# One core of Trainium2: a scan kernel whose B is broadcast over the partitions by one fp32 matmul in place of a bfloat16 matmul of three parts

## What is computed

```
u  = silu(conv4(x @ in_w_u) + conv_b)            # (512, 256)
z  = x @ in_w_z
dt8, B, C = split(u @ xproj_w.T)                 # (512, 8), (512, 16), (512, 16)
dt = softplus(dt8 @ dt_w.T + dt_b)               # (512, 256)
h[t, d, n] = exp(dt[t, d] * A[d, n]) * h[t-1, d, n] + dt[t, d] * B[t, n] * u[t, d]
y[t, d] = sum_n h[t, d, n] * C[t, n] + u[t, d] * D[d]
out = (y * silu(z)) @ out_w.T
```

## Time and profile before

| what | value |
|---|---|
| median of 3 runs | 493.03 us (490.91 to 496.62) |
| profiled execution | 496.12 us, span 494.3 us |
| mean granted TensorE clock | 0.914 of full speed |
| TensorE busy, matmuls | 410.5 us (83%) |
| VectorE busy | 422.3 us (85%) |
| ScalarE busy | 369.4 us (75%) |
| GpSimd busy | 404.3 us (82%) |

### The profile page before, as it was taken

The page is one execution under the profiler, slowest core; times in us unless marked ns, Lnnn a source line. Parts: engine busy times, 40 slices in busy tenths (PEclk is TensorE's granted clock), DMA queues, the critical chain, the costliest instruction groups (busy, mean ns, idle before and its releaser), DMA issues. The chain is left out here.

```text
span 494.3 us, 6553 instructions
## 1 busy us (share of the span) xinstructions
PE 410.5 (83%) x2200; PEld 276.7 (56%) x2200; DVE 422.3 (85%) x345; ACT 369.4 (75%) x719; POOL 404.3 (82%) x241
## 2 busy tenths in 40 slices
PE   1947995998699987989898998889998967798854
PEld 0335554664556574555655684555665845457643
DVE  3577997999989998988999879998999989899254
ACT  2298699679966969897889689898789786972040
POOL 1799689797988799988979899989899999958431
PEclk9967999998879998998999899999999895989778
DMA  8251242322241233222232314223322332210001
GB/s 238 87 196 46 86 110 82 110 85 91 64 146 47 90 108 107 86 91 65 85 108 100 112 50 107 86 92 106 108 86 107 79 106 93 70 42 2 0 1 42
DMA packets 17009, 43.48 MB, mean 88 GB/s; under 512 B 1616, under 2 KB 5968, under 8 KB 16976
## 3 DMA queue, kind: packets, MB, share of 16 engines
q1 hardware_dynamic: 16976, 43.06, 27.1%
HBM read 41.48 MB, written 1.57 MB: 87 GB/s over the span
## 5 line engine op out<-in xcount | busy, mean ns | idle before, releaser
L1020 POOL TENSOR_TENSOR hq<-hq,c_tiles 128x1024 f32<-128x1024 f32 x129 | 300.6, 2348 | 45.2 <-DVE hq L1147 42.7
L1147 DVE TENSOR_TENSOR_SCAN hq<-da,bb 128x1024 f32<-128x1024 f32 x113 | 255.9, 2280 | 10.0 <-PE bb L631 2.6
L650 PE MATMUL ysum<-wts,hq 128*128 128x128 f32 x1024 | 150.7, 295 | 18.5 <-POOL hq L1020 17.0
L816 ACT ACTIVATE da<-dt,neg_a 128x511 f32<-128x511 f32 x226 | 147.1, 711 | 7.1 <-DVE hq L1147 6.8
L650 PEld LDWEIGHTS ysum<-wts,hq 128*128 128x128 f32 x1024 | 122.9, 150 | 43.0 <-POOL hq L1020 24.3
L1128 DVE TENSOR_TENSOR bb<-bb,dtu 128x1024 f32<-128x1024 f32 x80 | 97.0, 1213 | 9.3 <-PE bb L604 5.8
L914 ACT ACTIVATE g<-dtu_t,bc_t 128x256 f32<-128x256 f32 x132 | 55.9, 497 | 0.0
L1147 DVE TENSOR_TENSOR_SCAN hq<-bb,dbu 128x1024 f32<-128x1024 f32 x15 | 34.3, 2286 | 13.4 <-ACT bb L827 6.3
L631 PE MATMUL bb<-wts,g 128*128 128x128 f32 x264 | 37.8, 290 | 9.1 <-ACT g L914 7.1
L631 PEld LDWEIGHTS bb<-wts,g 128*128 128x128 f32 x264 | 32.2, 150 | 18.5 <-issue 9.9
L604 PE MATMUL bb<-b_rows,pick 48*128 48x512 bf16 x76 | 30.4, 400 | 9.6 <-DVE hq L1147 9.6
(11 more groups left out here) (127 smaller groups left out, 500.1 us busy)
## 6 DMA issues: line engine op xcount, KB each, us to landing
c_tiles<-bc_rows_dram SPq DMA_DIRECT2D x64, 512.0 KB, 3.6
b_tiles<-bc_rows_dram SPq DMA_DIRECT2D x15, 256.0 KB, 4.4
wconv<-conv_taps_dram SPq DMA_DIRECT2D x2, 512.0 KB, 7.1
x_res<-x_dram SPq DMA_DIRECT2D x1, 768.0 KB, 9.2
out_dram<-o SPq DMA_DIRECT2D x3, 256.0 KB, 2.3
wts<-packed_dram SPq DMA_DIRECT2D x1, 584.0 KB, 10.2
hid<-w_ffn_dram SPq DMA_DIRECT2D x1, 576.0 KB, 8.6
bc_rows_dram<-xdbl SPq DMA_DIRECT2D x8, 64.0 KB, 3.1
```

The costliest lines, as they stand in the source:

```text
L650: mm = nc.tensor.matmul(ysum[:, h, block(b)], hq[:, i % H_RING, h, block(b)], ident, start=(first and b == 0), stop=(i % NS == NS - 1), is ...
L816: ins = nc.scalar.activation(da[:, i % DA_RING, h, 1:SEQ], dt[:, k % 2, h, 1:SEQ], ACT.Exp, scale=neg_a[:, c:c + 1])
L1020: nc.gpsimd.tensor_tensor(hq[:, i % H_RING, halves, :], hq[:, i % H_RING, halves, :], c_tiles[:, n % C_RING, i % 2, :].unsqueeze(1).broadc ...
L1147: nc.vector.tensor_tensor_scan(out=hq[:, i % H_RING].rearrange("p h t -> p (h t)"), data0=decay.rearrange("p h t -> p (h t)"), data1=dbu_t ...
```

## The change

`bcast` becomes, in all 80 plain steps, one fp32 matmul whose moving operand are the 16 rows of B in `xdbl` themselves, and whose stationary operand is column n of the first 16 rows of the fp32 identity, repeated 128 times. Stages `pick`, `split` and `b_rows` are gone on GpSimd, TensorE and ScalarE, with their tiles and semaphores, and so is the 16-column picker in the packed weights. `xdbl` now has two buffers, since the rows are read through the whole unit: the copy of unit k waits for the store of unit k-2 in place of k-1, and for the broadcasts of unit k-2.

```
                 if stage == "bcast":
                     i, = a
                     k, n = i // NS, i % NS
-                    if i == 0:
-                        was_read(pe, ("bc", k))
-                    if i == first_from_rows(k):
-                        was_read(pe, ("b_rows", k))
+                    was_read(pe, ("xproj", k))
                     if i >= BB_RING:
                         pe.wait_ge(s_scan, i - BB_RING + 1)
-                    if from_rows(i):
-
-                        mm = nc.tensor.matmul(bb[:, i % BB_RING, 1, :],
-                                              pick[0:PARTS * NS, n:n + 1].broadcast_to([PARTS * NS, P]),
-                                              b_rows[:, k % 2, :], start=True, stop=True)
-                    for b in () if from_rows(i) else range(BLK):
-                        mm = nc.tensor.matmul(bb[:, i % BB_RING, 1, block(b)],
-                                              bc_t[:, k % 2, b, ROW_B + n:ROW_B + n + 1].broadcast_to([P, P]),
-                                              ident, start=True, stop=True, is_transpose=True)
+                    mm = nc.tensor.matmul(bb[:, i % BB_RING, 1, :],
+                                          ident[0:NS, n:n + 1].broadcast_to([NS, P]),
+                                          xdbl[ROW_B:ROW_B + NS, k % 2, :], start=True, stop=True)
                     mm.then_inc(s_bcast, 1)
-                elif stage == "b_rows":
-                    k, = a
-                    pe.wait_ge(s_split, 4 * (k + 1))
-                    pe.wait_ge(s_pick, 1)
-                    may_write(pe, item)
-                    for b in range(BLK):
-                        mm = nc.tensor.matmul(scratch(item).bitcast(BF16)[0:PARTS * NS, block(b)],
-                                              b_parts[:, b].rearrange("p s n -> p (s n)"), ident16[:],
-                                              start=True, stop=True, is_transpose=True)
-                    signal_full(mm, item)
...
         if k == 0:
-            put(at, ("dtu_turn", 0, 0), ("dtu_turn", 0, 1), ("pick",), ("split", 0), ("turn", 0, 1))
-            put(at + 1, ("b_rows", 0))
+            put(at, ("dtu_turn", 0, 0), ("dtu_turn", 0, 1), ("turn", 0, 1))
...
-            put(at + then + 9, ("dt", n, 0), ("dt", n, 1), ("split", n), ("dtu", n))
+            put(at + then + 9, ("dt", n, 0), ("dt", n, 1), ("dtu", n))
...
-            put(at + (11 if ffn or k == 0 else 10), ("b_rows", n))
...
-                    if k >= 1:
-                        act.wait_ge(s_cst, 16 * k)
-                    signal_read(nc.scalar.activation(xdbl[0:XROWS, :], scratch(item)[0:XROWS, :], ACT.Copy), item)
+                    if k >= 2:
+                        act.wait_ge(s_cst, 16 * (k - 1))
+                        act.wait_ge(s_bcast, plain_steps(NS * (k - 1)))
+                    signal_read(nc.scalar.activation(xdbl[0:XROWS, k % 2, :], scratch(item)[0:XROWS, :], ACT.Copy), item)
...
-                elif stage == "split":
-
-                    k, = a
-                    was_read(pool, ("bc", k))
-                    if k >= 1:
-                        written(pool, ("b_rows", k - 1))
-                    b_t = bc_t[:, k % 2, :, ROW_B:ROW_B + NS]
-                    nc.gpsimd.tensor_copy(b_parts[:, :, 0, :], b_t).then_inc(s_split, 1)
...
```

More of the change, by code:

```diff
@@ L39 @@
 for _name, _n in (("ident", P), ("gamma", 1), ("beta", 1), ("conv_b", 4), ("skip", 4), ("a_log", 4 * NS),
-                  ("wx", 4 * XROWS), ("wdt", 2 * DI), ("rev", P), ("pick", NS), ("wz", 2 * DI), ("wo", 4 * DM)):
+                  ("wx", 4 * XROWS), ("wdt", 2 * DI), ("rev", P), ("wz", 2 * DI), ("wo", 4 * DM)):
     COLS[_name] = (_at, _at + _n)
@@ L47 @@
 G_RING = 2
-FIRST_ROWS = 4
-PARTS = 3
 TURNED = ((4, 6, 10, 13), (0, 4, 6, 10, 13)) + 3 * ((3, 6, 10, 13), (0, 5, 10, 13))
@@ L63 @@
 F32 = mybir.dt.float32
-BF16 = mybir.dt.bfloat16
 I32 = mybir.dt.int32
@@ L96, in plain_steps @@
     return i - turned_steps(i) - pooled_steps(i)
[L99 to L106, removed]
 def parts_of(q):
@@ L271 @@
 SCRATCH = (*(reader for reader, _ in PRODUCERS.values()), "turn", "z", "bc", "dt", "dtu_turn", "turn_x1",
-           "ffn_gate", "b_rows")
+           "ffn_gate")
 def plan_banks(order):
@@ L344, in mamba_sandwich @@
         zs = sb("zs", [P, 2, 2, SEQ])
-        xdbl = sb("xdbl", [P, SEQ])
+        xdbl = sb("xdbl", [P, 2, SEQ])
         bc_t = sb("bc_t", [P, 2, BLK, 2 * NS])
[L348 to L352, removed]
         dt = sb("dt", [P, 2, 2, SEQ])
@@ L399, in mamba_sandwich @@
         s_bcast = sem("b_broadcast")
-        s_pick = sem("row_picker_done")
-        s_split = sem("b_split_in_parts")
         s_g = sem("turned_dbu_made")
@@ L550, in _ @@
                 was_read(sp, ("xproj", k))
-                sp.dma_start(bc_rows[k], xdbl[0:2 * NS, :]).then_inc(s_cst, 16)
+                sp.dma_start(bc_rows[k], xdbl[0:2 * NS, k % 2, :]).then_inc(s_cst, 16)
                 sp.wait_ge(s_cst, 16 * (k + 1))
@@ L719, in _ @@
                     for b in range(BLK):
-                        mm = nc.tensor.matmul(scratch(item)[:, b * 2 * NS:(b + 1) * 2 * NS], xdbl[0:2 * NS, block(b)],
+                        mm = nc.tensor.matmul(scratch(item)[:, b * 2 * NS:(b + 1) * 2 * NS], xdbl[0:2 * NS, k % 2, block(b)],
                                               ident[0:2 * NS, 0:2 * NS], start=True, stop=True, is_transpose=True)
@@ L728, in _ @@
                     rows = slice(ROW_DT, XROWS + 1)
-                    signal_full(nc.tensor.matmul(scratch(item), wdt[rows, k % 2, h * P:(h + 1) * P], xdbl[rows, :],
+                    signal_full(nc.tensor.matmul(scratch(item), wdt[rows, k % 2, h * P:(h + 1) * P], xdbl[rows, k % 2, :],
                                                  start=True, stop=True), item)
@@ L876, in _ @@
                     written(act, item)
-                    if k >= 2:
-                        act.wait_ge(s_split, 4 * (k - 1))
                     signal_read(nc.scalar.activation(bc_t[:, k % 2].rearrange("p b n -> p (b n)"),
@@ L1117, in _ @@
         def _(dve):
-            nc.vector.memset(xdbl[ROW_DT:ROW_DT + 32, :], 1.0).then_inc(s_ones, 1)
+            nc.vector.memset(xdbl[ROW_DT:ROW_DT + 32, :, :], 1.0).then_inc(s_ones, 1)
             for item in ORDER:
@@ L1284 @@
     put("rev", np.eye(P, dtype=np.float32)[::-1])
-    put("pick", np.tile(np.eye(NS, dtype=np.float32), (P // NS, 1)))
     put("gamma", w["attn_gamma"])
```

## The result

The changed kernel takes 513.24 us (median of 4 runs, 512.75 to 515.16) where the kernel before takes 494.82 us (490.91 to 496.89) on the same chip: a ratio of 1.039, 95% interval 1.031 to 1.047. It is slower by 18 us; 504.2 was forecast. Its profiled execution took 513.25 us with a mean granted clock of 0.920, against 496.12 us and 0.914.

What follows compares the result with a forecast made beforehand. Three engines nearly fill the loop together, TensorE with little left. 14.1 us for units 1 to 6, plus 2 for unit 0, less 1.9 at the start and 3 of clock: +11.2, from 493.03 to 504.2 us; range 495 to 518.

Steps and rivals of the forecast that it cites:

- The 96% fill: Units 1 to 6: TensorE assumed to fill each unit to 96%, against 92% in the fullest unit now; +14.1 us.
- The count by slack: Second estimate, pairing broadcasts with their multiplies: 30 of 76 end under 0.7 us ahead, shortfalls 15.6 us; +12 to +20 us.
- the price of a broadcast: Each of 76 plain steps: the fp32 matmul holds TensorE 0.90 us against 0.32 for bf16, 44 us of work in all.
- The unit sums: TensorE's busy time per unit plus 0.58 us per broadcast less 0.49 for the turn; units 1 to 6 grow 14.1 us.
- The clock: Low-level time in units 1 to 6: a TensorE without gaps would have less of it, gaining 3 us (ends 0 and 16).
- rival 2: The clock recovers fully in units 1 to 6 and gives the loss back: 491 to 497 us, no change; chance 0.14.
- The chain's removal: Split, turn and copy of B's parts dropped: GpSimd's 1.1 us a unit counted as nothing, TensorE saves 0.49 us a unit.
- rival 3: Faster: the split's chain is worth more than the matmul, units shrink if GpSimd ends them; 485 us, 0.06 shared with Rival 4.
- The start: Steps 0 to 3: without the turn, step 3's multiply starts near 40.4 us in place of 42.28; 1.9 us gained.
- Unit 0's +2 us: Unit 0 has room on TensorE overall but not at each place, so 2 us were added.
- Rival 1: TensorE's queue becomes the bound outright with gaps as now: 519.5 us, or some 515 if the clock recovers; chance 0.15.
- Rival 4: The narrow matmul runs in one record at the old cost, only gains stay: 489 us; chance 0.06 shared with rival 3.

## Why the prediction missed

**The bound and the mechanism were right.** Against the 494.82 us of the same chip the forecast is +9.4 us and the measured time +18.4. TensorE was the engine with too little left; the time grew in units 1 to 6; VectorE's waits for the broadcast passed 15 us (29.6); TensorE stands at 94.5% or more in units 2 to 6; TensorE's waits for GpSimd's product fell from 17.0 us to 5.9. The 96% fill, a choice, measured 95.9%. The count by slack found 30 broadcasts short of 0.7 us; VectorE waited for 32.

**The term that failed is the price of a broadcast**, "I take 0.90, hence +0.58 us each". It measured 1.05 held and +0.73 on the cycle, outside the bound of 0.86 to 0.96. The bound came from dividing the dt pair's 1.91 us by two. Lone partial-row broadcasts show how that row should be split: two matmuls at the full-row price of 0.86 and 0.19 us once, for the change of rows. A broadcast stands alone between full-row matmuls and pays the 0.19 each time: 1.91 less 0.86 is 1.05. The sentence "that is 0.09 us for a pair of changes, and it lies inside my bound" failed with it, since the product of 1.82 us it compared with stood behind a partial-row broadcast or ahead of one and held a surcharge too: in full rows the same four records take 1.72. The Trainium skill (TensorEngine Tiling (Array Packing), Key Properties) says that a change of the tiling mode drains TensorE, and the prediction read its row as saying that this is small. The trace agrees that partial rows cost something, though no run shows that it is a drain: the runs show 0.34 us a step in the fp32 form, more than the old broadcast held; and 0.25 in the old form, so only 0.09 of it is new in the change.

With a us lost for each us held, as in the first half of unit 6, the 0.15 us too little make 0.7 us for its five broadcasts, and some 4 to 5 us over units 1 to 6 (an estimate); so much of the miss is the mis-sized price. The unit sums say the same: +14.1 forecast, +18.3 measured.

**The clock gave nothing.** The forecast had 3 us back, and rival 2 hung on it. The mean went from 0.914 to 0.920, and the time at the low level only from 66 to 64.5 us in the eight units, although TensorE is nearly always busy. Over 128 rows the fp32 broadcast has 17.6 us of it at a lower TensorE load. By the rule of the Trainium skill (TensorE: Matmul & The Clock Gate, Why this matters for your kernels), that the clock is kept where no longer gaps stand between matmuls, the changed kernel should have had more of it. The trace doesn't bear that out: from 113.0 to 126.3 us TensorE was busy for 13.24 of 13.30 us at the full clock, and it stood at the low level from 126.3 us to 133 us.

**The chain's removal** was "nothing" on GpSimd and 0.49 us of TensorE a unit. With the broadcast's hold unchanged it measured 5.9 us, and unit 6 shows 0.8 us of such a gain in its second half. So rival 3 was right that the chain is worth something; whether it comes through GpSimd, as the rival has it, or through the turn and the copy isn't shown, and it lacked the room that it asked for. GpSimd's busy time fell by 7.8 us (9 forecast).

**The start** came out near its forecast by luck. The 1.9 us were for the multiply of step 3, which is at 38.61 and not 42.28. Of these 3.7 us, 2.1 are the first scan's, and the forecast had no such term; it is as large as the scatter of single executions. The kernel with z moved, whose start is the changed kernel's, has its first scan at 29.17, and the kernels with the repeated bf16 matmul, whose start is the one before, at 28.34 to 30.24. From the first scan the multiply of step 3 gained 1.6 us. In the timeline of the changed kernel:

```profile
35.07 1.23 DVE L1058 TENSOR_TENSOR bb<-bb,dtu 128x1024 f32<-128x1024 f32 x1 [1.58 <-PE bb L575]
...
38.61 1.21 DVE L1058 TENSOR_TENSOR bb<-bb,dtu 128x1024 f32<-128x1024 f32 x1
...
47.12 1.23 DVE L1058 TENSOR_TENSOR bb<-bb,dtu 128x1024 f32<-128x1024 f32 x1 [2.34 <-PE bb L575]
```

By step 5 only 0.9 us of the lead is left (48.06 before), eaten by the wait for a broadcast. Unit 0's +2 us measured +2.2.

**The books.** Against the profiled execution +11.2 was forecast and 17.1 measured: 4.2 in units 1 to 6, 3 of clock, 0.2 in unit 0, less 0.2 at the start and 1.2 in unit 7 and the tail. The rest of the 9 us is the base: the forecast took off 3.1 us because the one profiled execution lay above its median; that of the changed kernel lies on it.

**The rivals.** Rival 1 (TensorE outright, 515 to 520) is nearest in time, but not for its reason: it kept the gaps as they were, and they shrank. Rival 2 fell with the clock (0.87 to 1.00 in units 1 to 6, not 0.98 or more), rival 3 with the price. Rival 4 fell: two records in every one of the 80 broadcasts.

**Left open.** Why the clock stays low in this kernel with partial rows. The bf16 kernel in 128 rows stays at 0.912 with a less busy TensorE, so full rows alone don't raise it; the fp32 kernel in 64 rows is at 0.943, between; and the bf16 matmul three times has 0.903 to 0.912 where two and four times have 0.915 to 0.927. What the low clock costs in all wasn't measured. Also, TensorE's busy time in units 1 to 6 rose by 34.9 us where 59 broadcasts by 0.73 less the turns make 40; how far that is the busy column's way of counting wasn't tried.

## What to carry to other kernels

Price a matmul by where it stands: take the start-to-start cycle of the whole step on the timeline, not a record's length or a group's time divided by its members, add these up over the stretch with all its kinds of steps, and hold the sum against that of the engine that sets the pace; up to it extra work costs little, above it each tenth costs in full (1.07 us for five times 0.215). Look for a stretch at full clock before reading a law from totals. A partial-row matmul between full-row ones should be padded to all 128 rows with zeros, or replaced by transposes of a column if its data are at hand in the other layout: here the padding alone turned 1.039 into 0.983, by less time held and by a higher clock, and the transposes made the fastest versions, 0.962 with 478.7 us (0.965 with the dt projection in full rows as well). Room on an engine counts in the half of the unit where the new work falls, and idle time behind a chain isn't room.

## What the hardware showed that was not expected

- A lone fp32 matmul of 16 or of 64 rows and 512 columns among full-row ones holds TensorE for 1.05 us, of 128 rows for 0.86; the fold and taps behind it take 0.15 us longer too. In bf16 it is 0.32 against 0.21.
- An fp32 broadcast of 512 columns holds 0.86 us as one matmul and 0.44 us as four transposes.
- From 45 to 445 us the clock is 0.99 in the kernels with the fp32 broadcast over 128 rows, with and without idle transposes, 0.97 with four transposes, 0.96 over 64 rows and 0.94 over 16. The bf16 broadcast over 128 rows has 0.93, so it isn't the rows alone.
- Two matmuls on different rows ran at the same time: the dt projection and the broadcast, in TensorE's timeline of the changed kernel:

```profile
69.42 0.69 PE L686 MATMUL scr<-xdbl,wts 9*128 9x512 f32 x1
69.43 0.69 PE L575 MATMUL bb<-xdbl,wts 16*128 16x512 f32 x1
69.95 0.59 PE L686 MATMUL scr<-xdbl,wts 9*128 9x512 f32 x1
69.96 0.59 PE L575 MATMUL bb<-xdbl,wts 16*128 16x512 f32 x1
```

In each pair the second started 0.01 us behind the first, where elsewhere the next matmul waits 0.53 us for the first one's record.
